# A two-layer kernel's prologue: identity multiplications on TensorE, a smaller context load, and loads and splits in another order

## The reference

```python
out = conv1d(x, weight, padding=4, groups=4)         # 64 channels, 9 taps
ctx = einsum('nd,od->no', cond_128, c_weight)        # context, 128 -> 64
y = out + ctx[:, :, None] + side[None, :, None]
base = einsum('bsi,oi->bso', y, base_w) + base_b     # 1024 -> 1024
# plus a top-2-of-16 expert part with rank-64 factors; router and
# factor A are 80 more output columns over y
x = x + base + delta * 0.5
```

## Time and profile before

| | before |
|---|---|
| median of 3 runs | 1286.2 us (1284.76 to 1287.85) |
| profiled execution | 1286.09 us, span 1284.2 us |
| TensorE (PE) busy | 1247.4 us, 97% |
| VectorE (DVE) busy | 639.1 us, 50% |
| ScalarE (ACT) busy | 375.5 us, 29% |
| GpSimd (POOL) busy | 272.6 us, 21% |
| mean granted TensorE clock | 0.993 |

### The profile page before, as it was taken

How to read it: one execution, slowest core, us unless ns; L and a number is a source line. 1 busy time by engine, 2 the same in 40 slices (tenths; PEclk the granted TensorE clock), 3 DMA queues, 4 the chain that set the end, 5 groups by cost and what they waited for, 6 DMA issues and landing times.

```text
span 1284.2 us, 22374 instructions
## 1 busy us (share of the span) xinstructions
PE 1247.4 (97%) x7333; PEld 1105.9 (86%) x7333; DVE 639.1 (50%) x1811; ACT 375.5 (29%) x801; POOL 272.6 (21%) x306
## 2 busy tenths in 40 slices
PE   6998999999999999998799999999999999999998
PEld 6998999999899999998578878788788888888887
DVE  6666666666444445455634424334253453453452
ACT  4312222121242433422333333443322222222221
POOL 2222222222222222234211121111121211211200
PEclk9999999999999999999899999999999999999999
DMA  7346655333899999968689999999855455445410
GB/s 278 120 149 226 203 193 180 124 103 104 227 304 317 287 297 292 297 248 212 130 182 287 289 259 304 247 295 290 269 131 99 114 115 98 114 114 98 114 49 33
DMA packets 84898, 250.22 MB, mean 195 GB/s; under 512 B 27521, under 2 KB 32001, under 8 KB 77570
## 3 DMA queue, kind: packets, MB, share of 16 engines
q1 hardware_dynamic: 72320, 213.34, 52.2%
q0 software_dynamic: 11264, 35.66, 16.1%
q10 hardware_dynamic: 1266, 0.70, 0.2%
HBM read 154.24 MB, written 95.42 MB: 194 GB/s over the span
## 4 chain that ended last, share of the span: by engine, by line
PE 49%; DMA 2%; DVE 1%; SPq 0%; issue 0%; ACT 0%; POOL 0%; ACTq 0%; POOLq 0%
PE z L1307 13%; PE z L1308 13%; PE z L1309 13%; PE t L1429 2%; DMA xin<-zs_dram,gpos 2%; PE c L1372 1%; PE c L1308 1%; PE c L1307 1%; PE c L1309 1%; PE c L1376 1%; PE prep L1546 1%; DMA bd<-bd_dram 1%; PE c L1374 1%; PE t L1374 0%; SPq L427 0%
## 5 line engine op out<-in xcount | busy, mean ns | idle before, releaser
L1307 PE MATMUL z<-w_1h,yh 128*128 128x384 f32 (+1 forms) x512 | 192.5, 376 | 0.5 <-DVE w_1l L1034 0.5
L1307 PE MATMUL z<-w_0h,yh 128*128 128x384 f32 (+1 forms) x512 | 190.1, 371 | 0.0
L942 DVE TENSOR_TENSOR yl<-t,yh 128x512 fp32r<-128x512 f32 x128 | 82.4, 685 | 215.2 <-ACT yh L704 215.2
L1308 PE MATMUL z<-w_1h,yl 128*128 128x384 f32 (+1 forms) x512 | 188.0, 367 | 0.0
L1309 PE MATMUL z<-w_1l,yh 128*128 128x384 f32 (+1 forms) x512 | 187.9, 367 | 0.0
L1308 PE MATMUL z<-w_0h,yl 128*128 128x384 f32 (+1 forms) x512 | 187.1, 365 | 0.0
L1309 PE MATMUL z<-w_0l,yh 128*128 128x384 f32 (+1 forms) x512 | 187.1, 365 | 0.0
L638 POOL TENSOR_TENSOR carrier<-ones_col 128x1 f32<-128x1 f32 x96 | 21.4, 223 | 702.2 <-DVE den L1008 230.7
L1307 PE MATMUL z<-w_2h,yh 128*128 128x336 f32 (+1 forms) x512 | 153.6, 300 | 8.8 <-DVE den L1008 5.0
L1308 PE MATMUL z<-w_2h,yl 128*128 128x336 f32 (+1 forms) x512 | 153.0, 299 | 0.0
L1309 PE MATMUL z<-w_2l,yh 128*128 128x336 f32 (+1 forms) x512 | 152.9, 299 | 0.0
(11 more groups left out here) (219 smaller groups left out, 2411.1 us busy)
## 6 DMA issues: line engine op xcount, KB each, us to landing
bd<-bd_dram SPq DMA_DIRECT2D x96, 512.0 KB
zs_dram<-zt SPq DMA_DIRECT2D x96, 512.0 KB, 7.4
x8raw<-in_x_dram SPq DMA_DIRECT2D x32, 516.0 KB, 4.3
xin<-in_x_dram SPq DMA_DIRECT2D x32, 512.0 KB
x_dram<-xb SPq DMA_DIRECT2D x32, 512.0 KB, 5.3
out_dram<-xb SPq DMA_DIRECT2D x32, 512.0 KB
bd_dram<-bd SPq DMA_DIRECT2D x8, 1024.0 KB
xin<-x_dram SPq DMA_DIRECT2D x16, 512.0 KB
```

What stands on the lines that cost most here:

```text
L942: V.tensor_tensor(o, v, y_places(s, yh, b)[0], ALU.subtract).then_inc(s.y_lo[b], 1)
L1307: T.matmul(o, ah, wh, start=start, stop=False, **kw)
L1308: T.matmul(o, al, wh, start=False, stop=False, **kw)
```

## The change

1. TensorE waits for the finished identity and multiplies it by itself 8 times (`warm(8)`, full float32, 128 columns, into bank z0, whose content is not used), before the context matmuls, and 8 times more after them.
2. The context matrix comes as 128 x 64 (32 KB in place of 256 KB), and VectorE spreads it to `ctxrep` with one 128 x 512 copy; TensorE waits for that too.
3. ScalarE makes a 128 x 1 copy after its three context loads. The other nine loads (`load_mlp`) are issued behind `w0_high(1)` of tile 0.
4. SyncE issues w0 of bank 0 ahead of x and `bias0b`, and w0 of bank 1 ahead of x8 of tile 1.
5. ScalarE splits two pieces of w0 of bank 0 ahead of `y_high(0)`. VectorE does one piece of `w0_low(2)` ahead of `conv_out(0)`, two between it and `y_low(0)`, and the last behind `y_low(0)`.

```diff
@@ sync
-                if b == 2:
+                if b == 0:
                     load_x(0, 0)
                     sp.dma_start(bias0b[:, :], row(bias0, P)).then_inc(bias0_in, 16)
-                if b == 0:
-                    load_x8(1)
+            load_x8(1)
             load_x(0, 1)
@@ gpsimd
-            nc.gpsimd.memset(ident[:, :], 0.0).then_inc(id_zero, 1)
-            pool.wait_ge(id_zero, 1)
+            nc.gpsimd.memset(ident[:, :], 0.0).then_inc(id_ready, 1)
+            pool.wait_ge(id_ready, 1)
@@ scalar
-            act.dma_start(ctxrep[:, :, :].rearrange("p g c -> p (g c)"), ctx_in).then_inc(cond_in, 16)
+            act.dma_start(ctxw[:, :, :].rearrange("p g c -> p (g c)"), ctx_in).then_inc(cond_in, 16)
             act.dma_start(siderep[:, :, :].rearrange("p g c -> p (g c)"), side_in_order).then_inc(cond_in, 16)
-            for j, (w, b) in enumerate(((cW0, cb0), (cW1, cb1))):
...
+            act.wait_ge(ones_ready, 2)
+            copy(carrier[:, :], ones_col[:, :])
+
+            def load_mlp():
+                for j, (w, b) in enumerate(((cW0, cb0), (cW1, cb1))):
+                    act.dma_start(cw[j][:, :], w).then_inc(mlp_in, 16)
+                    act.dma_start(cbias[j][:, :], b.rearrange("(n a) -> n a", a=1)).then_inc(mlp_in, 16)
...
+                act.dma_start(mixT[:, :, :].rearrange("p k o -> p (k o)"), mix_in_order).then_inc(mixw_in, 16)
...
             w0_high(2, 0, W0_PIECES)
+            w0_high(0, 0, 2)
             y_high(a0, 0, 0)
             y_high(a0, 0, 1)
-            w0_high(0, 0, W0_PIECES)
+            w0_high(0, 2, W0_PIECES)
             x8_high(1)
...
                 if first:
                     w0_high(1, 0, W0_PIECES)
+                    load_mlp()
@@ vector
+            dve.wait_ge(cond_in, 16 * 3)
+            V.tensor_copy(ctxrep[:, :, :, :], ctxw[:, :, :].unsqueeze(2).to_broadcast([P, GROUPS, BLK, CI])).then_inc(ctx_spread, 1)
             for w in range(2):
                 dve.wait_ge(th_ready, w + 1)
...
-            w0_low(2, 0, W0_PIECES)
+            w0_low(2, 0, 1)
             conv_out(0)
+            w0_low(2, 1, 3)
             y_low(a0, 0)
+            w0_low(2, 3, W0_PIECES)
             w0_low(0, 0, W0_PIECES)
@@ tensor
+            def warm(n):
+
+                for _ in range(n):
+                    T.matmul(z[0][:, 0:P], ident[:, :], ident[:, :], start=True, stop=True)
+
+            pe.wait_ge(id_ready, 2)
+            warm(8)
             pe.wait_ge(cond_in, 16 * 3)
+            pe.wait_ge(ctx_spread, 1)
             pe.wait_ge(ones_ready, 2)
...
             mm.then_inc(ctx_ps, 1)
-            pe.wait_ge(id_ready, 1)
+            warm(8)
             pe.wait_ge(tl_ready, 2)
             conv(0)
             turn_conv(0)
```

More of the change, by code:

```diff
@@ L256, in build @@
         condT = sb(s, "condT", [P, NS])
-        ctxrep = sb(s, "ctxrep", [P, GROUPS, BLK * CI])
+        ctxw = sb(s, "ctxw", [P, GROUPS, CI])
+        ctxrep = sb(s, "ctxrep", [P, GROUPS, BLK, CI])
         siderep = sb(s, "siderep", [1, GROUPS, BLK * CI])
@@ L270, in build @@
         x1 = xin + [x1_2, x1_3]
-        id_zero, id_ready, iota_ready = sem("id_zero"), sem("id_ready"), sem("iota_ready")
+        id_ready, iota_ready, ctx_spread = sem("id_ready"), sem("iota_ready"), sem("ctx_spread")
         ones_ready = sem("ones_ready")
@@ L707, in _ @@
             act.dma_start(condT[:, :], condT_in).then_inc(cond_in, 16)
-            act.dma_start(ctxrep[:, :, :].rearrange("p g c -> p (g c)"), ctx_in).then_inc(cond_in, 16)
+            act.dma_start(ctxw[:, :, :].rearrange("p g c -> p (g c)"), ctx_in).then_inc(cond_in, 16)
             act.dma_start(siderep[:, :, :].rearrange("p g c -> p (g c)"), side_in_order).then_inc(cond_in, 16)
-            for j, (w, b) in enumerate(((cW0, cb0), (cW1, cb1))):
[L711 to L717, removed]
+            act.wait_ge(ones_ready, 2)
[4 more added lines that the diff above has]
+                    act.dma_start(cbias[j][:, :], b.rearrange("(n a) -> n a", a=1)).then_inc(mlp_in, 16)
+                act.dma_start(w2[:, :], cW2).then_inc(mlp_in, 16)
+                act.dma_start(b2b[:, :], row(cb2, NS)).then_inc(mlp_in, 16)
+                for s in range(2):
+                    act.dma_start(mixbias[:, s, :], mix_b).then_inc(mlp_in, 16)
+                act.dma_start(mixT[:, :, :].rearrange("p k o -> p (k o)"), mix_in_order).then_inc(mixw_in, 16)
             def x8_high(t):
@@ L1406, in _ @@
                 o = z[2][:, NS * g:NS * (g + 1)]
-                T.matmul(o, ctxrep[:, g, :], condT[:, :], start=True, stop=False)
+                T.matmul(o, ctxrep[:, g, :, :].rearrange("p j c -> p (j c)"), condT[:, :], start=True, stop=False)
                 mm = T.matmul(o, siderep[:, g, :], ones[:, :], start=False, stop=True)
             mm.then_inc(ctx_ps, 1)
-            pe.wait_ge(id_ready, 1)
+            warm(8)
             pe.wait_ge(tl_ready, 2)
@@ L1607 @@
                     toep[:, a, w, :, j, :] = taps[:, :, :, BLK * w + a - j].transpose(2, 0, 1)
-    ctx_w = _np.broadcast_to(v["L0_cond_c_weight"].T.reshape(P, GROUPS, 1, CI), (P, GROUPS, BLK, CI))
     side = _np.broadcast_to(v["fside_S_0"].reshape(1, GROUPS, 1, CI), (1, GROUPS, BLK, CI))
@@ L1616 @@
         "x": v["x"], "x8": x8.reshape(TILES, P, NG, NB + 1), "toeplitz": toep.reshape(P, 2 * GROUPS * BLK * CI),
-        "condT": v["cond_128"].T, "ctx": ctx_w.reshape(P, GROUPS * BLK * CI), "side": side.reshape(1, GROUPS * BLK * CI),
+        "condT": v["cond_128"].T, "ctx": v["L0_cond_c_weight"].T, "side": side.reshape(1, GROUPS * BLK * CI),
         "w0": w0.reshape(P, KC, L + AR), "bias0": v["L0_ffn_base_b"], "b0": b0,
```

## The result

The changed kernel takes 1291.63 us in the median of 17 runs (1288.75 to 1296.29), the one before 1286.73 on the same chip: a ratio of 1.0037, with a 95% interval of 1.0024 to 1.0050. That is slower by 0.4%, where I had forecast 1283.6 us and a range to 1288.0. The profiled execution took 1289.36 us around a span of 1287.6.

What follows compares the result with a forecast made beforehand. TensorE, busy 97% of the span, was taken as the bound. A sweep 3.0 us earlier (3.3 won, 0.3 lost on VectorE), less 0.4 behind it, leaves 2.6: 1283.6 us, range 1281.9 to 1288.0.

Steps and rivals of the forecast that it cites:

- The operands: Before conv(0): an earlier table load lets `th` start at 6.0 to 6.7 us, operands ready at 9.5 to 10.2.
- The first fillers: TensorE ahead of the context matmuls: `warm(8)`, sixteen instructions, starts at 1.7 us and takes 3.9, to 5.6 us.
- the upper bound: Longest estimate for eight fillers at the slow clock: 0.73 us a pair, 5.8 us in all.
- The context part: TensorE's context matmuls from 5.6 us: 3.2 us, between 4.9 slow and about 2.3 fast, ending at 8.8.
- The second fillers: Eight multiplications between context matmuls and conv(0): 1.8 us at the fast clock, so conv(0) starts at 10.6 us.
- late-clock rival: Short fillers, slow context part: conv(0) starts at 13.9 us and ends where it did; about 1286.5 us, chance 0.12.
- the rival of the fillers in the way: Fillers at their upper bound, clock low: conv(0) at 18.2 us, 6.3 late; 1292.0 us, slower; chance 0.14.
- conv(0) at 0.12 us: First dense convolution on TensorE: 24 matmuls at the fast clock take 2.9 us, ending at 13.6 instead of 16.9.
- The order on VectorE: Between conv(0) and first sweep: two weight pieces, 1.7 us, mostly fill a wait and cost 0.3; sweep at 17.7 us.
- the rival in which GpSimd holds VectorE: GpSimd's addition blocks the moved weight pieces: 0.5 us won to 1.8 lost, 1286.8 us in the middle; chance 0.10.
- Behind the sweep: After the first sweep: late `w0_low(1)` (0 to 1.0 us) and x8 split (0 to 1.4) together cost 0.4 us.
- The rest of the program: After the prologue: a microsecond won there is kept if each engine feeding TensorE moves forward too.

Runs made afterwards that it cites:

- gap16: The changed kernel without its two filler groups, with sixteen fillers behind the first tile's convolution and transposes (`warm(16)` behind `turn_conv(0)`); ratio 1.0018.
- after_third: The changed kernel, unedited, profiled a third time; no separate time given.
- grouped: old_splits_no_second with the four context matmuls of 128 rows first, then the four of one row, sharing a PSUM bank; sweep at 19.20 us, time not given.
- old_splits_no_second: The changed kernel with all four `w0_low(2)` pieces ahead of `conv_out(0)` and without the second fillers; sweep at 20.98 us, time not given.
- no_second: The changed kernel without the eight fillers behind the context matmuls; ratio not given, its interval overlaps that of the changed kernel.
- fill_only: The kernel before with both groups of eight fillers and nothing else; ratio 1.0040.
- old_splits: The changed kernel with VectorE's old order, all four pieces of `w0_low(2)` ahead of `conv_out(0)`, both filler groups kept; time not given.
- after_again: The changed kernel, unedited, profiled a second time; conv(0) began at 14.05 us, no separate time given.
- fill_gap: The changed kernel with seven more fillers behind `turn_conv(0)`, in TensorE's wait for `yl`; time not given.
- first16: The changed kernel with all sixteen fillers ahead of the context part and none behind it; median 1289.42 us, ratio not to be told from 1.
- banks_fill: The changed kernel with grouped context sums in four banks, old splitting order, `warm(11)` ahead, none behind the context part, `warm(4)` behind `turn_conv(0)`; 0.18% faster than before.
- no_fill: The changed kernel without either group of fillers; slower than the kernel before by 0.18%.

## Why the prediction was wrong

**The operands: right, and better.** The table load starts at 2.31 us, `th` at 5.87, a little below my lower bound of 6.0, and conv(0)'s operands were there at 9.23. The spread took 0.43 us and did not hold `tl`; it did hold the context part (below).

**The first fillers: right.** 3.78 us for sixteen instructions, 0.21 apart behind the first, as in my lower bound; I had 3.9. At the fast clock they are 0.11 apart in gap16, which makes the 1.8 us that I had. (One slip in the upper bound: 6.86 to 11.94 us are 0.635 us a pair. The 0.62 is right, as the part ends before conv(0) starts.)

**The context part: the step that failed.** I wrote "the context matmuls, 4.9 us slow or about 2.3 fast, I put at 3.2, the clock rising early in them", from 5.6 us on. Three things were off. The three loads landed at 6.20 us, though they were 66 KB in place of 290, and not near 5; the spread came behind them, and the context part started at 6.72 (1.1 us of the sum). Between 5.47 and 6.72 TensorE stood idle. And the part ran at 0.62 us a pair, 4.9 us (1.7 more): in after the clock rose at 14.74 us only. Nine profiles have eight fillers ahead of this part. In four of them (after, after_third, grouped, old_splits_no_second) the clock did not rise before 14.1 us. In four (no_second, fill_only, old_splits, after_again) it rose at 4.6 to 5.3 and fell again at 8.0 to 8.7, in the midst of the context matmuls. In fill_gap it was up from 6.08 to 9.49, nearly to the part's end. Of all profiles in which it rose this early, first16, which has no idle time ahead of the part, is the only one in which it stayed up through conv(0); banks_fill has none either, and there it fell at 10.17. So what keeps the clock is not settled. And a fast part takes 2.8 to 2.9 us (first16, fill_gap), not the 2.3 that I halved it to. I had a row that spoke against me and named it in a rival: before the change, the same matmuls had gone 5 us without a rise.

**The second fillers: 3.3 us in place of 1.8.** This follows from the step before, and 1.5 us of the sum with it. So conv(0) starts 4.3 us later than forecast: 1.1 + 1.7 + 1.5. This is the late-clock rival (13.9 us) with the late landing on top, and beyond the 13.5 us from which I had the fillers decide. Its time of 1286.5 us was not met either, as conv(0), though fast, ended 1.2 us later than before, and the losses behind it were not in it. That the rival of the fillers in the way, priced at 1292.0 us, is so near the measured 1291.6 is luck: it had each filler at its upper bound of 0.73 us and conv(0) at 18.2, and they took 0.41 to 0.47 us and conv(0) started at 14.9. Its sentence on the queue, that all stand ahead of conv in one queue, is what happened.

**conv(0) at 0.12 us: right.** It ends at 18.03, 1.2 us later than before.

**The order on VectorE: right about after, wrong in weight.** In after it costs nothing (0.3 forecast): from the second extraction of conv(0) to `yl` are 2.15 us, 2.13 before. But it is a second barrier behind the first, the rival in which GpSimd holds VectorE: where conv(0) ends sooner, at 15.7 to 16.6 us (no_second, fill_gap, gap16, no_fill), the pieces come beside GpSimd's addition and take 2.9 to 3.8 us. In first16 they are over before it. The two instructions of no_second that overlap agree with the Trainium skill, "SBUF — State Buffer", section "Who interferes with whom", which has the later of the two block; the 3.83 us in place of 1.61 and the 1.61 behind the addition are what the rule gives.

**Behind the sweep: wrong.** I had 0.4 us of loss and no fall of the clock. first16, the kernel that has the sweep where I forecast it, loses 1.9 us there against before; 1.5 of it are longer waits, for `w_1l` (1.3 us) and `x8l`. After has a stretch at half clock at 21.6 us in two profiles and at 23.4 in the third, behind the 1.9 us for `yl`; the first sweep loses 1.4 us by it, in the first profile. ScalarE's nine issues cost nothing there: they ran beside its own copies of `w_1h`. In one profile of three before has such a stretch too.

**The rest of the program: wrong.** I took every microsecond of the prologue as kept, because TensorE is busy 97% of the span. first16 shows that it is not: 1.65 us sooner than before at conv(2), by 37.67, and 3.1 us longer in its span. What comes later, about 2.5 us in the means above, was in no term of my sum.

Shown by experiment is that the fillers alone cost as much as the change (fill_only), and, by each kernel's one profile, the second barrier (no_second, the three with the old order). Read from profiles only are the slow context part and the clock's part in the sweep; they differ from one execution of a program to the next. Open are what keeps the clock up and the causes of the later loss.

## What to carry to other kernels

Work that is put in to keep TensorE busy must not stand between ready operands and the work that waits for them: sixteen fillers, half of them there, cost as much as the whole change. Placed so that they reach until the inputs land, the same sixteen brought conv(0) to the forecast start in the one profile taken, and no gain in time. Follow a microsecond won at the start to the end of the span before counting it: here it was lost again at late transfers, at a slow stretch near 661 us and at the last store. Where two hindrances stand one behind the other, take out both before calling either cheap. And compare several profiles of each kernel before reading 3 us at one place: two executions of one program differed by that much in where their clock fell.

## What the runs showed of the hardware

- Matmuls without a gap between them need not keep the clock: pairs of full float32 matmuls of 64 columns, alternating between 128 rows and one row, ran back to back from 6.75 to 10.64 us in no_second, and the granted clock fell at 8.14 in their midst. It had risen at 4.73 in the same run, within identity matmuls of 128 columns.
- A change between 128 rows and one row costs time: four full float32 matmuls of each in turn take 4.9 us in old_splits_no_second, and grouped 3.76 us in the kernel grouped, at the slow clock in both.
- A full float32 matmul of 128 columns (two instructions) takes 0.41 to 0.47 us at the slow clock (eight in 3.28 and in 3.78 us in after) and 0.23 at the fast one (sixteen in 3.74 us in gap16).
- A start flag on a second sum in one PSUM bank, set before the first sum is finished, changed the sums of the kernel grouped; in banks of their own they stay whole.
- ScalarE's queue issued nine transfers between 29.5 and 33.6 us while it copied weights, whose starts stayed 0.74 us apart, as they are in before, which has none there.
- A store of 512 KB that nothing else follows landed 2.58 us behind its issue in fill_only and 3.55 us in after, and each of these two values stands, to 0.01 us, in a whole group of profiles; what decides between them is open.
